# A decoder kernel: the first attention's output weights scaled on ScalarE, and one product of the weights' four-bit rounding made on GpSimd

## What is computed

```python
def _L0_attn_ref(x, q, k, log_decay, norm_weight, o_w):
    ...
    o = jnp.moveaxis(o, 0, 1).reshape(b, n, dm)
    o = o * jax.lax.rsqrt(jnp.mean(o * o, axis=-1, keepdims=True) + EPS) * norm_weight
    return o @ o_w.T

def fp4_quant_dequant(x):          # blocks of 16 along the last dimension
    ...
    scale = jnp.max(jnp.abs(xb), axis=-1, keepdims=True) / 6.0
    scale = jnp.maximum(scale, jnp.float32(1e-12))
    xn = xb / scale
    idx = jnp.searchsorted(_MID, jnp.abs(xn))
    q = _GRID[idx] * jnp.sign(xn) * scale
    return q.reshape(shape)
```

## Time and profile before

| | |
|---|---|
| median of three runs | 996.41 us (993.87 to 996.79) |
| profiled execution | 998.28 us |
| its span, from the first to the last instruction | 995.2 us |
| mean granted TensorE clock | 0.95 |
| busy: TensorE, VectorE, ScalarE, GpSimd | 868.6, 615.4, 497.9, 297.1 us |

### The profile page before, as it was taken

The page is one execution under the profiler, slowest core; times in us unless marked ns, Lnnn a source line. Parts: engine busy times, 40 slices in busy tenths (PEclk is TensorE's granted clock), DMA queues, the critical chain, the costliest instruction groups (busy, mean ns, idle before and its releaser), DMA issues.

```text
span 995.2 us, 19709 instructions
## 1 busy us (share of the span) xinstructions
PE 868.6 (87%) x7316; PEld 688.7 (69%) x7316; DVE 615.4 (62%) x1840; ACT 497.9 (50%) x1159; POOL 297.1 (30%) x478
## 2 busy tenths in 40 slices
PE   3669899999999899999999999999999999299950
PEld 2446668667777666777678777877877888289940
DVE  4998776676765768866848685778854434200016
ACT  2335446553656454553465545565555555045535
POOL 4423322222343123431213333232421214212236
PEclk9679999999999989999999999999999999689985
DMA  8996000000010000000000030231121226699836
GB/s 323 400 323 210 2 1 12 12 7 17 17 33 28 18 7 17 22 22 17 6 2 22 23 118 23 91 118 54 55 84 54 92 91 212 225 318 351 321 129 235
DMA packets 35950, 102.33 MB, mean 103 GB/s; under 512 B 4984, under 2 KB 20352, under 8 KB 35296
## 3 DMA queue, kind: packets, MB, share of 16 engines
q1 hardware_dynamic: 32448, 91.74, 27.0%
q0 software_dynamic: 3408, 9.34, 2.5%
HBM read 87.53 MB, written 33.35 MB: 121 GB/s over the span
## 4 chain that ended last, share of the span: by engine, by line
PE 63%; DVE 19%; ACT 7%; issue 6%; DMA 3%; POOL 1%; SPq 0%; ACTq 0%; DVEq 0%; POOLq 0%
PE ps L705 44%; PE ps L710 7%; PE ps L717 5%; PE ps L781 3%; DVE PT L1104 2%; DVE stat L1045 2%; ACT PT L1438 2%; ACT slot_rows L1438 1%; PE ps L848 1%; DMA xs_d<-X,idx 1%; PE ps L1006 1%; DVE sm L1061 1%; DVE PT L1069 1%; DMA KB<-xs_d 1%; DVE stat L1046 1%
## 5 line engine op out<-in xcount | busy, mean ns | idle before, releaser
L1626 POOL TENSOR_TENSOR stat<-stat,mhalf 128x1 f32<-128x1 f32 x112 | 67.1, 599 | 291.2 <-DVE stat L1047 291.1
L705 PE MATMUL ps<-wall,slot_rows 128*128 128x256 f32 (+1 forms) x448 | 132.3, 424 | 11.3 <-ACT KB L1465 8.9
L705 PEld LDWEIGHTS ps<-wall,slot_rows 128*128 128x128 f32 x448 | 79.1, 193 | 36.0 <-issue 22.8
L710 PE MATMUL ps<-cst,PT 128*128 128x128 f32 x512 | 73.4, 280 | 14.9 <-DVE PT L1104 4.2
L717 PE MATMUL ps<-KB 32*128 32x128 f32 (+1 forms) x2048 | 76.9, 287 | 7.2 <-DVE PT L1104 2.4
L1104 DVE TENSOR_REDUCE PT<-ps 128x8 f32<-128x1024 f32 x64 | 75.3, 1219 | 12.5 <-PE ps L717 12.4
L705 PE MATMUL ps<-wgu,slot_rows 128*128 128x352 f32 x256 | 82.1, 473 | 0.8 <-ACT slot_rows L1400 0.6
L717 PEld LDWEIGHTS ps<-KB 32*128 32x128 f32 (+1 forms) x2048 | 64.9, 190 | 25.7 <-issue 20.6
L705 PEld LDWEIGHTS ps<-slot_rows,wall 128*128 128x128 f32 x640 | 75.8, 193 | 8.5 <-issue 4.1
L705 PE MATMUL ps<-slot_rows,wall 128*128 128x128 f32 x640 | 79.6, 279 | 1.8 <-DVE KB L1165 0.9
L710 PEld LDWEIGHTS ps<-cst,PT 128*128 128x128 f32 x512 | 58.7, 143 | 30.6 <-issue 16.2
(11 more groups left out here) (237 smaller groups left out, 1817.5 us busy)
## 6 DMA issues: line engine op xcount, KB each, us to landing
EW<-moe_w SPq DMA_DIRECT2D x23, 514.0 KB, 4.3
EW<-moe_w SPq DMA_DIRECT2D x23, 512.0 KB, 5.0
PT<-moe_w SPq DMA_DIRECT2D x12, 514.0 KB, 5.9
PT<-moe_w SPq DMA_DIRECT2D x12, 512.0 KB, 6.9
wall<-wts SPq DMA_DIRECT2D x1, 4104.0 KB, 20.4
work<-xs_d SPq DMA_DIRECT2D x25, 129.0 KB, 3.3
KB<-ys_d SPq DMA_DIRECT2D x8, 384.0 KB, 5.9
slot_rows<-ys_d SPq DMA_DIRECT2D x8, 384.0 KB, 9.3
```

What stands on the lines that cost most here:

```text
L705: last = k.e.matmul(o, a, b, start=(i == 0), stop=(i == len(pairs) - 1))
L710: last = k.e.transpose(ps[:, u.at, c * P:(c + 1) * P], src[:, c * P:(c + 1) * P], ident)
L1626: return k.e.tensor_tensor(v[:, 7:8], v[:, 8:9], mhalf[:, :], ALU.pow)
```

## The change

The two products with `par` move from `dve_start` to `act_start`, where ScalarE waits for the first weights and a new semaphore `par_ready`. In the weights' rounding, the product of the weights with the reciprocal moves from VectorE to GpSimd, which waits for a new semaphore `wri_ready`, raised by the reciprocal; ScalarE's magnitude waits for the GpSimd product as it did for VectorE's. The activations' rounding is untouched. The planner's costs of a weight part's first piece follow.

```diff
 def plan_weights():
     for i in range(9):
-        yield piece(work=[("D", 2.07, None), ("A", 0.63, ("abs", i))], needs=[("w4", i // 4), *[("wq", i - 2)] * (i > 1)],
+        yield piece(work=[("D", 1.45, None), ("P", 1.1, None), ("A", 0.63, ("abs", i))], needs=[("w4", i // 4), *[("wq", i - 2)] * (i > 1)],
                     alone=True)
         yield piece(work=[("D", 1.4, None), ("P", 1.2, ("wq", i))],
                     needs=[("abs", i)])
...
-        def dve_fp4_head(k, src, n, tmp, small, xn_sem):
+        def dve_fp4_scales(k, src, n, small):
             e, m = k.e, n // DH
             am, sc, ri = (small(j)[:, 0:m] for j in range(3))
             k.after(k.step(e.tensor_reduce(am, v3(src, DH), AX.X, ALU.max, apply_absolute_value=True)))
             k.after(k.step(e.tensor_scalar(sc, am, SIXTH, 1e-12, ALU.mult, ALU.max)))
-            k.after(k.step(e.reciprocal(ri, sc)))
+            return e.reciprocal(ri, sc)
+
+        def dve_fp4_head(k, src, n, tmp, small, xn_sem):
+            e, m = k.e, n // DH
+            ri = small(2)[:, 0:m]
+            k.after(k.step(dve_fp4_scales(k, src, n, small)))
             e.tensor_tensor(v3(tmp[0], DH), v3(src, DH), bc(ri.unsqueeze(2), m, DH), ALU.mult).then_inc(xn_sem, 1)
...
                 if i >= 2:
                     k.wait_ge(wq_odd if i % 2 else wq_even, i // 2)
-                dve_fp4_head(k, part, width, tmp, small, wxn_ready)
+                dve_fp4_scales(k, part, width, small).then_inc(wri_ready, 1)
                 yield
...
             k.wait_ge(emptied[u.at], u.out)
-            k.after(k.step(e.tensor_tensor(par[:, 4:6], par[:, 2:4], c_("nw"), ALU.mult)))
-            k.wait_ge(ld_w[0], 16)
-            for c in range(2):
-                e.tensor_scalar(oT[:, c, :], oT[:, c, :], par[:, 4 + c:5 + c], None, ALU.mult).then_inc(oT_ready, 1)
+            e.tensor_tensor(par[:, 4:6], par[:, 2:4], c_("nw"), ALU.mult).then_inc(par_ready, 1)
...
         def act_start(k):
             k.wait_ge(ld_col, 16)
             k.e.activation(lam[:, :], c_("ld"), ACT.Exp, scale=-1.0).then_inc(lam_exp, 1)
+            oT = v3(w("oT"), D)
+            k.wait_ge(ld_w[0], 16)
+            k.wait_ge(par_ready, 1)
+            for c in range(2):
+                k.e.activation(oT[:, c, :], oT[:, c, :], ACT.Identity, scale=par[:, 4 + c:5 + c], bias=0.0).then_inc(oT_ready, 1)
...
         def pool_weights(k):
             for i, (f, lo, width) in enumerate(wq_parts):
-                yield
                 m = width // DH
-                part, y = v3(raw[f][0][:, lo:lo + width], DH), v3(wq_part(i, width)[1], DH)
+                part, (xn, y) = raw[f][0][:, lo:lo + width], wq_part(i, width)
+                k.wait_ge(wri_ready, i + 1)
+                k.e.tensor_tensor(v3(xn, DH), v3(part, DH), bc(ws[:, i % 2, 2, 0:m].unsqueeze(2), m, DH),
+                                  ALU.mult).then_inc(wxn_ready, 1)
+                yield
                 k.wait_ge(wy_ready, i + 1)
-                k.e.tensor_tensor(part, y, bc(ws[:, i % 2, 1, 0:m].unsqueeze(2), m, DH), ALU.mult).then_inc(
-                    wq_odd if i % 2 else wq_even, 1)
+                k.e.tensor_tensor(v3(part, DH), v3(y, DH), bc(ws[:, i % 2, 1, 0:m].unsqueeze(2), m, DH),
+                                  ALU.mult).then_inc(wq_odd if i % 2 else wq_even, 1)
                 yield
```

More of the change, by code:

```diff
@@ L599, in decoder_kernel @@
         vector, scalar, gpsimd = sems("vector"), sems("scalar"), sems("gpsimd")
-        wxn_ready, wabs_ready, wy_ready, wq_even, wq_odd = (sem(n) for n in (
-            "wxn_ready", "wabs_ready", "wy_ready", "wq_even", "wq_odd"))
+        wri_ready, wxn_ready, wabs_ready, wy_ready, wq_even, wq_odd = (sem(n) for n in (
+            "wri_ready", "wxn_ready", "wabs_ready", "wy_ready", "wq_even", "wq_odd"))
         lg_ready, pr_ready, picked, idx_ready, tab_ready, directed, redirected, placed, halved, joined, var6, centred, root6, out_ready = (
@@ L606, in decoder_kernel @@
                              "halved", "joined", "var6", "centred", "root6", "out_ready"))
+        par_ready = sem("par_ready")
         gated = sem("gated")
@@ L1382, in dve_start @@
         def dve_start(k):
-            e, u, oT = k.e, start_fill, v3(w("oT"), D)
+            e, u = k.e, start_fill
             k.wait_ge(lam_exp, 1)
@@ L1722, in pool_weights @@
             for i, (f, lo, width) in enumerate(wq_parts):
+                m = width // DH
+                part, (xn, y) = raw[f][0][:, lo:lo + width], wq_part(i, width)
+                k.wait_ge(wri_ready, i + 1)
+                k.e.tensor_tensor(v3(xn, DH), v3(part, DH), bc(ws[:, i % 2, 2, 0:m].unsqueeze(2), m, DH),
+                                  ALU.mult).then_inc(wxn_ready, 1)
                 yield
-                m = width // DH
-                part, y = v3(raw[f][0][:, lo:lo + width], DH), v3(wq_part(i, width)[1], DH)
                 k.wait_ge(wy_ready, i + 1)
-                k.e.tensor_tensor(part, y, bc(ws[:, i % 2, 1, 0:m].unsqueeze(2), m, DH), ALU.mult).then_inc(
-                    wq_odd if i % 2 else wq_even, 1)
+                k.e.tensor_tensor(v3(part, DH), v3(y, DH), bc(ws[:, i % 2, 1, 0:m].unsqueeze(2), m, DH),
+                                  ALU.mult).then_inc(wq_odd if i % 2 else wq_even, 1)
                 yield
```

## The result

The changed kernel took 1017.29 us (1014.61 to 1021.44, four runs) against 996.0 us for the kernel before: a ratio of 1.0228, 95% interval 1.0206 to 1.0251. It is 21 us slower; I had forecast 994.5, in a range of 986 to 1002. The profiled execution took 1015.93 us, with a span of 1013.5.

What follows compares the result with a forecast made beforehand. It took VectorE to bound the ramp (20 to 80 us) and TensorE the middle (100 to 850 us). Minus 1.2 us at the start and minus 0.7 for GpSimd's product gave 994.5 us by the median, range 986 to 1002.

Steps and rivals of the forecast that it cites:

- The first product: Kernel start: TensorE's first product of sample 0 was to start near 7.45 us, not 9.71, 2.25 us earlier.
- the key and value products: Kernel start: held by the weights' second piece, they were to start 1.6 us earlier than 16.72, near 15.1.
- The lead of 1.2 us on VectorE: Kernel start: moving the output weights to ScalarE was to start the ramp 1.2 us earlier, bounds 0.3 to 1.6.
- the walk: Weights' rounding: stepping through VectorE's present order, stalls behind nine GpSimd products came to 5.4 us against 5.6 saved.
- the four lines that I had named: Ramp: VectorE's lines 1091, 1095, 1056 or 1062 behind GpSimd products would take 0.8 to 1.5 us, not 0.2 to 0.56.
- The 1.9 us of my sum: Whole kernel: the forecast gain, 1.2 us from the start and 0.7 from the product on GpSimd.
- whole gain: Ramp: rival in which GpSimd's product costs VectorE nothing and 1.2 + 5.6 us reach the end, 989.6 us; chance 0.26.
- the 0.7 us of gain that I had: Weights' rounding: forecast gain from moving the product to GpSimd, between a gain of 5.6 and a loss of 3.7.
- The new order changes the middle: 100 to 875 us: rival in which the new list shifts TensorE's idle by 5.6 us, 989 or 1000; chance 0.18.
- The dear-lock rival: Weights' rounding: each GpSimd product holds VectorE its full 1.06 us, 998.9, or 1001.6 with idle tails; chance 0.20.

Runs made afterwards that it cites:

- both_d200: The changed kernel, both moves kept, on the list written with a planned VectorE cost of 2.0: 992.14 us, ratio 0.9961.
- edits_old_list: The changed kernel with the planner's old costs, so both moves on the list of the kernel before: 996.02 us, ratio 0.9999.
- list_alone: The kernel before with only the changed kernel's planner costs (VectorE 1.45, GpSimd 1.1), no instruction moved: 1016.9 us, ratio 1.0214.
- list_d200: The kernel before with the planner's VectorE cost at 2.0 instead of 2.07, no instruction moved: 993.89 us, ratio 0.9978.
- the fillers: The changed kernel with 47 useless identity products on TensorE in 14 places where it waits for data: 1010.08 us, ratio 1.015.

## Why the prediction was wrong

**What bounds the kernel.** Right, and not used to its end. I read that TensorE bounds 750 of the 995 us, and that a lead from the ramp lasts only "if the long middle is filled as well as now". The edit to the planner's costs reaches every microsecond of that middle. I worked out the two moves to tenths of a microsecond and gave the middle one sentence.

**The start.** The first product was forecast near 7.5 us and came at 7.22; the key and value products were forecast near 15.1 and came at 15.35. The lead of 1.2 us on VectorE did not come: it went on at 20.43 in the changed kernel and 20.23 with this move alone, against 20.42. The failed term is the time from those products to VectorE's first use of them, which I had carried over from the kernel before as 3.7 us (16.72 to 20.42). It measured 5.1 us in the changed kernel and 4.3 with this move alone. TensorE begins these products at its lower level, and an earlier start doesn't bring an earlier end of it: their weight loads are 0.85 us apart up to 18.22 in the kernel before and up to 18.89 in the changed one. That end scatters. With both moves the spacing lasts to 17.83 in the profile of `both_d200`, where VectorE goes on at 19.55, and to 19.01 in that of `edits_old_list`, where it goes on at 20.71. The other profiles with this move lie between 20.23 and 20.71, so the lead stands in one of seven, each of one execution.

**The product on GpSimd.** Right in kind and near in size, as far as single profiles say. VectorE's groups from 20 to 80 us, first of the kernel before, then of the changed kernel (count, busy us, mean ns):

```profile
L1091 DVE TENSOR_TENSOR PT<-slot_rows,cst 128x256 f32<-128x256 f32 x6 | 2.6, 439 | 0.0
L1135 DVE TENSOR_TENSOR_SCAN slot_rows<-lam,Y 128x128 f32<-128x128 f32 x6 | 2.4, 448 | 0.0
L1146 DVE SCALAR_TENSOR_TENSOR slot_rows<-slot_rows,sm 128x256 f32<-128x256 f32 x2 | 1.0, 478 | 0.0
```

```profile
L1097 DVE TENSOR_TENSOR PT<-slot_rows,cst 128x256 f32<-128x256 f32 x6 | 4.8, 799 | 0.0
L1141 DVE TENSOR_TENSOR_SCAN slot_rows<-lam,Y 128x128 f32<-128x128 f32 x6 | 3.1, 562 | 0.0
L1152 DVE SCALAR_TENSOR_TENSOR slot_rows<-slot_rows,sm 128x256 f32<-128x256 f32 x3 | 2.8, 939 | 0.4 <-POOL sm L1679 0.4
```

Line 1097 (1091 in the kernel before) waits behind GpSimd's product: 1.22 us at 22.58, beside a product that runs from 22.46 to 23.52.

```profile
22.46 1.06 POOL L1734 TENSOR_TENSOR work<-EW,X 128x512 f32<-128x512 f32 x1 [0.74 <-DVE X L1064]
22.58 1.22 DVE L1097 TENSOR_TENSOR PT<-slot_rows,cst 128x256 f32<-128x256 f32 x1
```

These three groups pay 2.2, 0.7 and 1.4 us more ((799 - 439) x 6, (562 - 448) x 6, (939 - 478) x 3), 4.3 in all, where the walk had 5.4 for all lines. The lists differ too, so this is a measure of size only. Of the four lines that I had named, 1091 alone shows it in its mean; 1056 rises by 0.07 us, and 1095 and 1062 don't rise. VectorE waited 2.1 us for ScalarE's absolute value, where the kernel before waited 1.7. The last rounding part's tail begins at 74.11, 1.4 us later than before (72.66), but this compares two lists. On one list, the two moves bring it from 75.69 to 74.11 (`list_alone` and the changed kernel), from 73.32 to 71.21 (`list_d200` and `both_d200`), and from 72.66 to 72.98 (the kernel before and `edits_old_list`). The 1.9 us of my sum are about what the ramp gave in two of the three, and the "whole gain" rival, which needs over 4 us, is refuted in all. With the old list the product's move came to 0.999 (0.9966 to 1.0013), which holds the 0.7 us of gain that I had and also nothing. The Trainium skill, *SBUF — State Buffer*, "SBUF: two separate sides", describes an exclusive lock on the port pair, held for the whole instruction, and the 1.22 us agree with it. Its price here is about the product's.

**The rivals.** The step that made the forecast wrong is that the sum, minus 1.2 and minus 0.7, has no term for the middle: it took the 33.7 us of idle and the clock of 0.99 over into a kernel with another list. The new list alone costs 21 us (1016.9 against 996). The idle of the middle rose by a third, to 44.5 us, and the low clock cost as much again. "The new order changes the middle" was the right rival, with a chance of 0.18 split evenly between gain and loss, and a size of 5.6 us, "a sixth" of the idle, with the clock named but not priced. Nor was an even split right: of six other lists one was faster by 2 us, two were level and three were 8 to 21 us slower, though six are few. The dear-lock rival would have put the loss in the ramp, which is unchanged.

**The marks I had set.** "TensorE idle from 100 to 850 us other than 33.7 by over 3 us would say that the list made the time": it is 44.5, and it did.

**What stays open.** What in the changed kernel's list makes TensorE idle longer I didn't trace to single choices of the planner, nor did I part the order of the pieces from the banks that the planner hands out with it. The 7 us of the fillers are measured, for 17 us less at the lower level; the 13.8 of the account are worked out for all of it; no run held the clock up and left the rest as it was.

## What to carry to other kernels

Where a planner or scheduler writes the order, an edit to its costs is a change to the whole kernel: time the new order without the edit, and the edit on the old order, before believing either. One order over another is worth up to 23 us here, the two moves at most some 2 us on one order. Moving a two-tensor product from VectorE to GpSimd frees little while VectorE's next work also reads two SBUF tensors: here 0.999, within 0.9966 to 1.0013.

## What the runs showed of the hardware

Short idle stretches are dear to a bound TensorE twice: 32 instructions took 1.17 us and, after 1.89 and 1.63 us of idle, 2.09 us, and filling such waits with useless products gained 7 us of 1017. The clock shown for the first 20 us is 1.00 in both kernels, yet the 128x512 instructions starting at 15.35 us in the changed kernel come 0.85 us apart (the weight loads at 16.34, 17.19 and 18.04). That is the spacing of the lower level: four of them took 3.60 us at 39.22 in the kernel before, where the clock is 0.50, and 1.88 us at 192.06 in the changed kernel, where it is 1.00. In `list_alone` and `list_d200`, with the same spacing, the column shows 0.91 for the first 20 us. At the very start of these profiles the clock column can't be trusted; the spacing of equal instructions can.
